# Complement masks of five tiles of a graph attention head made by accumulating DMAs, a new order of tiles on TensorE, and a fourth comparison on VectorE in every other head

## What is computed

```python
seq = (x @ W_seq).reshape(N, H, DH)                     # N = 2048, H = 16, DH = 32
score1 = jnp.einsum('nhd,d->hn', seq, a1)
score2 = jnp.einsum('nhd,d->hn', seq, a2)
scores = leaky_relu(score1[:, :, None] + score2[:, None, :], negative_slope=0.2)
scores = scores + (1.0 - adj)[None, :, :] * MASK_VAL
attn = softmax(scores, axis=-1)
hidden = jnp.einsum('hij,jhd->ihd', attn, seq).reshape(N, D_IN)
x = x + elu(hidden @ W_out + b_out)
```

## Time and profile before

| | |
|---|---|
| median of 3 runs | 1165.29 us (1164.87 to 1166.19) |
| the profiled execution | 1169.42 us, span of its instructions 1167.0 us |
| heads of the second layer | from about 635 to 1096 us of the span |
| busy share of the span, PE, DVE, ACT, POOL | 93%, 81%, 69%, 14% |

### The profile page before, as it was taken

How to read it: one execution, slowest core, us unless ns; L and a number is a source line. 1 busy time by engine, 2 the same in 40 slices (tenths; PEclk the granted TensorE clock), 3 DMA queues, 4 the chain that set the end, 5 groups by cost and what they waited for, 6 DMA issues and landing times. The chain is left out here.

```text
span 1167.0 us, 24746 instructions
## 1 busy us (share of the span) xinstructions
PE 1080.7 (93%) x10565; PEld 738.8 (63%) x10565; DVE 949.3 (81%) x1323; ACT 809.0 (69%) x843; POOL 163.1 (14%) x174
## 2 busy tenths in 40 slices
PE   1999986999999999999996999999999999999997
PEld 1444432444444444444443999999999999999743
DVE  2355336899999999998834899999999999999565
ACT  1334326677777777775525999999999999999122
POOL 2788640000000000000000100100110000000011
PEclk9999996999999999999997899999999999999999
DMA  9630452322221121000433011110111111111311
GB/s 340 142 26 2 110 104 68 75 57 66 66 66 43 42 57 57 28 37 27 163 126 131 38 38 38 38 39 38 38 38 38 39 38 38 38 39 38 110 72 72
DMA packets 38269, 77.69 MB, mean 67 GB/s; under 512 B 5653, under 2 KB 15250, under 8 KB 36114
## 3 DMA queue, kind: packets, MB, share of 16 engines
q1 hardware_dynamic: 31954, 67.62, 16.1%
q0 software_dynamic: 6208, 8.50, 6.0%
HBM read 65.39 MB, written 23.21 MB: 76 GB/s over the span
## 5 line engine op out<-in xcount | busy, mean ns | idle before, releaser
L1443 ACT ACTIVATE area_h<-area_a,keep 128x2048 fp8e4<-128x2048 f32 x208 | 396.9, 1987 | 0.5 <-PEq L1577 0.5
L1595 PE MATMUL psum<-s_V,area_h 128*128 128x99 bf16 x2560 | 254.5, 210 | 21.1 <-issue 10.9
L1595 PEld LDWEIGHTS psum<-s_V,area_h 128*128 128x128 fp8e4 x2560 | 237.4, 98 | 25.2 <-issue 22.8
L1598 PE MATMUL psum<-s_V,area_h 128*128 128x198 bf16 x1536 | 218.7, 249 | 0.0
L1599 PE MATMUL psum<-s_V,late 128*128 128x99 bf16 x1536 | 212.8, 209 | 0.0
L1596 PE MATMUL psum<-s_V,area_b 128*128 128x99 bf16 x2048 | 205.5, 210 | 0.0
L1596 PEld LDWEIGHTS psum<-s_V,area_b 128*128 128x128 fp8e4 x2048 | 190.3, 98 | 0.0
L737 PE MATMUL psum<-area_h,f_region 128*128 128x512 f32 x384 | 184.9, 596 | 0.0
L1493 DVE TENSOR_TENSOR area_h<-area_h,area_a 128x512 uint32<-128x512 uint32 x256 | 173.5, 688 | 9.1 <-ACT area_h L1443 4.6
L1159 DVE SCALAR_TENSOR_TENSOR f_region<-area_b,s_r,f_region 128x1500 f32<-128x1500 f32 x96 | 170.8, 1780 | 2.2
L1170 DVE CUSTOM_DVE_ANT_0 area_b<-psum,late 128x1500 f32<-128x1500 f32 x96 | 161.1, 1715 | 10.8 <-PE psum L652 10.6
(11 more groups left out here) (175 smaller groups left out, 1343.5 us busy)
## 6 DMA issues: line engine op xcount, KB each, us to landing
area_a<-s_rows SPq DMA_DIRECT2D x16, 1024.0 KB, 4.6
rel_planes<-f_h SPq DMA_DIRECT2D x3, 2304.0 KB, 15.9
late<-rel_planes SPq DMA_DIRECT2D x36, 192.0 KB, 2.6
area_h<-in_x SPq DMA_DIRECT2D x4, 1024.0 KB, 12.9
keep<-in_adj POOLq DMA_DIRECT2D x16, 256.0 KB, 6.6
f_region<-in_x SPq DMA_DIRECT2D x16, 256.0 KB, 4.7
x<-f_region SPq DMA_DIRECT2D x16, 256.0 KB, 2.0
area_a<-adj_chunks SPq DMA_DIRECT2D x4, 1024.0 KB, 9.1
```

What stands on the lines that cost most here:

```text
L1443: act.activation(masks[:, j, :], s1b[:, b, :], ACT.Relu, bias=t["s2"][:, n, 0, j:j + 1], scale=BIG, saturate=False).then_inc(signs, 1)
L1595: pe.matmul(out[:, :, 0:DZ], masks[:, j, cols], V[:, b, j, :, 0:DZ], **first)
L1598: pe.matmul(out, masks[:, j, cols], V[:, b, j, :, :], **first)
```

## The change

The set FAR of tiles with a complement of their own grows from ten to twelve. Five of them (0, 2, 6, 8, 11) no longer get it from VectorE: a plain copy of the adjacency tile is laid out in `fars`, and GpSimd issues a DMA that adds the mask to it as 16-bit integers. 0x40 + 0x40 = 0x80 in a byte is minus zero, 0x40 + 0 stays 2.0, so the sum is the complement. Since the DMA overwrites the copy, SP loads it anew for each head from memory (`far_rows`), once TensorE has used the tile (begin_far). VectorE makes the complements of tiles 1, 7, 9, 12 and 14, GpSimd those of 3 and 5 as before. TensorE takes the tiles in the order of TURN instead of 0 to 15; the mask of tile j is still made in the order of j. In odd heads VectorE compares four tiles (2, 6, 10, 14) instead of three. The stage ahead writes four tiles of `nadjT` and five copies of adjacency tiles, and SP stores those five to `far_rows`.

```diff
+            for d, j in enumerate(DMA_FAR):
+                sp.wait_ge(t["apart"], d + 1)
+                sp.dma_start(t["far_rows"][d], t["fars"][FAR.index(j)]).then_inc(t["far_begun"][d], 16)
             heads.sync(sp)
...
             dve.wait_ge(masked, HA * ET)
+            dve.wait_ge(w_ready, ET)
             for i, j in enumerate(NEAR_TILES):
                 dve.tensor_scalar(t["nadjT"][:, i, :].bitcast(U32).rearrange("p (t i) -> p t i", t=NT),
                                   t["adjT"][:, :, j, :].bitcast(U32), SIGNS, None, ALU.bitwise_xor).then_inc(t["lasting"], 1)
+            for j in DMA_FAR:
+                dve.tensor_scalar(t["fars"][FAR.index(j)].bitcast(U32).rearrange("p (t i) -> p t i", t=NT),
+                                  t["adjT"][:, :, j, :].bitcast(U32), 0, None, ALU.bitwise_or).then_inc(t["apart"], 1)
...
-VECTOR_SIGN = (3, 8, 13)
-FAR = (0, 1, 3, 5, 6, 7, 9, 11, 13, 14)
+SIGN_TILES = ((3, 8, 13), (2, 6, 10, 14))
+FAR = (1, 3, 5, 7, 9, 12, 14, 0, 2, 6, 8, 11)
 POOL_FAR = (3, 5)
-VECTOR_FAR = tuple(j for j in FAR if j not in POOL_FAR)
+DMA_FAR = (0, 2, 6, 8, 11)
+VECTOR_FAR = tuple(j for j in FAR if j not in POOL_FAR + DMA_FAR)
+TURN = (1, 3, 4, 5, 0, 7, 2, 9, 10, 12, 6, 13, 8, 14, 15, 11)
...
-            for n in range(HB - 2):
-                sp.wait_ge(mask_ready, NT * (n + 1))
-                load(n + 2, n % 2)
+
+            def begin_far(n, d):
+
+                place = TURN.index(DMA_FAR[d])
+                if place < NT - 1:
+                    sp.wait_ge(mask_used, (NT - 1) * (n + 1) + place + 1)
+                else:
+                    sp.wait_ge(psum_done[1], n + 1)
+                sp.dma_start(fars[FAR.index(DMA_FAR[d])], t["far_rows"][d]).then_inc(far_begun[d], 16)
+            for n in range(HB - 1):
+                for d in range(len(DMA_FAR) - 1):
+                    begin_far(n, d)
+                if n < HB - 2:
+                    sp.wait_ge(mask_ready, NT * (n + 1))
+                    load(n + 2, n % 2)
+                begin_far(n, len(DMA_FAR) - 1)
...
-                for j in POOL_FAR:
+                for j in sorted(POOL_FAR + DMA_FAR):
                     pool.wait_ge(mask_ready, NT * n + j + 1)
-                    complement(pool, j, ALU.subtract).then_inc(pool_far, 1)
+                    if j in POOL_FAR:
+                        complement(pool, j, ALU.subtract).then_inc(pool_far, 1)
+                    else:
+                        d = DMA_FAR.index(j)
+                        pool.wait_ge(far_begun[d], 16 * (n + 1))
+                        pool.dma_start(fars[FAR.index(j)].bitcast(U16), masks[:, j, :].bitcast(U16), accum_op=ALU.add).then_inc(far_added[d], 16)
...
-                    if j not in VECTOR_SIGN:
-
-                        if j < NT - 1:
-                            act.wait_ge(mask_used, (NT - 1) * n + j + 1)
+                    if j not in SIGN_TILES[n % 2]:
+
+                        if TURN.index(j) < NT - 1:
+                            act.wait_ge(mask_used, (NT - 1) * n + TURN.index(j) + 1)
                         elif n > 0:
                             act.wait_ge(psum_done[1], n)
...
-                    if j + 1 in VECTOR_SIGN:
+                    if j + 1 in SIGN_TILES[n % 2]:
                         vector_sign(n, b, j + 1)
...
-            def step(n, b, half, j):
-
-                base = 4 * half
-                if j == 0:
+            def step(n, b, half, place):
+
+                base, j = 4 * half, TURN[place]
+                if place == 0:
                     pe.wait_ge(bank_free[half], n + 1)
                 pe.wait_ge(mask_ready, NT * n + j + 1)
                 if j in POOL_FAR:
                     pe.wait_ge(pool_far, len(POOL_FAR) * n + POOL_FAR.index(j) + 1)
+                elif j in DMA_FAR:
+                    pe.wait_ge(far_added[DMA_FAR.index(j)], 16 * (n + 1))
                 elif j in FAR:
                     pe.wait_ge(far_ready, len(VECTOR_FAR) * n + VECTOR_FAR.index(j) + 1)
```

## The result

The changed kernel takes **1177.16 us** (median of 4 runs, 1175.48 to 1180.18), the kernel before 1165.08 beside it (1164.46 to 1166.19): a ratio of 1.0097, 95% interval 1.0069 to 1.0126. The forecast was 1171.5 in a range of 1164 to 1179, slower. The sign and the path that sets a head's time came true. The forecast's own sum was 6.25 us, so 5.8 of the 12.1 us were not in it.

The account below looks back on a forecast made before the run. VectorE's work sum bounded the kernel at 28.21 us a head; after the change a loop of 28.51, taken as 28.535, would. First head, fourteen loops (399.49) and last head gave 6.25 later: 1165.29 + 6.25 = 1171.5 us, range 1164 to 1179.

Parts of the forecast that it names:

- the loop over tile 12's complement: Second reduction, VectorE's way to that complement, TensorE's remaining steps, next second reduction: 28.51 us a head; forecast's chance 0.66.
- rival (d): In the heads, VectorE's operations lengthen beside five times the DMA traffic: 5% is 0.6 us a head, 1180; chance 0.06.
- second path: First half's full PSUM, first reduction and masks delay the second reduction: 0.03 to 0.05 us more in half the heads.
- TensorE's gaps: Waits on VectorE's complements: about 1.2 us at place 5 (even heads), 1 at 7 (odd), 1.3 to 1.5 at 9.
- Rival (a): Engines' work sums set the heads, 0.8 to 1.2 us less each: 1148 to 1154 us; chance 0.13.
- tile 7's loop: Even heads, from second reduction over tile 7's complement and TensorE's remaining steps to the next: 27.27 us.
- tile 9's loop: From second reduction over tile 9's complement and TensorE's remaining steps to the next: 26.99 us.
- The accumulating DMA: GpSimd's mask-adding DMA in the heads: taken as 6.6 us, free up to 11.7, no gain from landing early.
- What follows it is not changed: Everything behind the last reduction, up to the kernel's end, was claimed to take the same time: nothing added.
- Head 0: First head, no reductions: TensorE waits for tile 12's complement; second reduction at 676.82 instead of 675.89.
- Head 15: Last head, no take-offs: 10.36 + 0.82 + 14.79 + 0.20 = 26.17 us to the last reduction.
- Stores and copies in the stage ahead: Before the heads, VectorE's three more copies and SP's five stores: costed at nothing, perhaps a microsecond or two once.

Follow-up runs that it names:

- reduce_later: Changed kernel with VectorE's second reduction behind mask 7 of the next head instead of mask 5; 1186.00 us, ratio 1.0156 to the kernel before.
- the swap: Changed kernel with only tiles 12 and 6 exchanged in TensorE's order; 1158.32 us, ratio 0.9926 to the kernel before.

## Why the prediction was right, and where it was short

- **Which path sets the head: right.** No engine's sum, but the loop over tile 12's complement. Forecast 12.70 + 0.82 + 14.79 + 0.20 = 28.51; measured 12.82 (857.66 - 844.84), 0.82 (to 858.48) and 14.98 (to 873.46), 28.62, and 28.60 on average. Fourteen heads: 399.49 forecast, 400.40 measured. The 0.12 in the first term is one comparison of 1.40 us instead of 1.28. Ten comparisons of this trace begin 0.2 us after GpSimd has begun to issue a DMA, and all ten take 1.39 to 1.44; 24 others meet an issue otherwise and keep 1.28. That is rival (d) in small, by the issue and not by the traffic.
- **Not seen: the loop through the first reduction**, 28.68, which ties with it. The forecast had it only as a "second path" that costs 0.03 to 0.05. The time came out the same, but advice drawn from the one loop alone (reduce_later) promised at least twice what both loops leave.
- **TensorE's gaps: right in place**, at 5 in even heads, 7 in odd ones and 9 in both, and nearly so in size: 1.10 for about 1.2, 0.88 for about 1, and at place 9 1.35 in odd and 1.09 in even heads for 1.3 to 1.5. VectorE idles 1.93 us in one head and 0.89 in the next, forecast 2.1 and 0.9.
- **Rival (a), the sums decide, is excluded** by the changed kernel, **and is nearly what the swap gives**, 27.36. But the forecast had its two halves wrong. It gave 27.27 in even heads, by tile 7's loop, and 27.60 in odd ones. In the swap it is 27.60 from an even head to an odd one, by VectorE's sum, which is above tile 7's loop there, and 27.15 from an odd head to an even one, by tile 9's loop (forecast 26.99).
- **The accumulating DMA: bounded rightly.** Landing took 3.5 us, where the value taken was 6.6 and the room 12.3. In the order of the change no step waited for it; in the order 0 to 15 it was late. The estimate of 3.8 worked out from the Trainium skill (DMA: Bandwidth & Descriptors, Anatomy of one DMA — SWDGE (gpsimd) path) was the nearer. The warning of the Trainium skill (SBUF — State Buffer, SBUF: two separate sides) about GpSimd's descriptors is borne out in kind and not in size: ten of the eighty issues grew from 0.86 to 1.70 us and ended 0.1 us after the comparison that they met, none to five times its length. The prediction took 0.6 us for an issue; nothing in this order hung on the difference.

```profile
late<-area_h POOLq DMA_DIRECT2D x64, 256.0 KB, 3.5
```

```profile
848.98 1.70 POOL L1454 DMA_DIRECT2D late<-area_h  x1 [0.33 <-DVE area_h L1525]
```

- **"What follows it is not changed": wrong, 4.2 us.** The instructions are not, but GpSimd's closing drain depends on how many DMAs it issued in its last block (since its drain at 577 us in before and at 571 in after). This is the largest part of the miss, a term that the sum put at nothing.
- **Head 0: 0.93 forecast, 0.99 where the clock held**, and 1.6 more where TensorE's clock fell after its stop; the rest of its 3.8 is the wait for the row of s1, which the kernel before has too when its stage ahead ends on time.
- **Head 15**: 26.17 forecast, 26.38 measured. **Stores and copies in the stage ahead**: no cost found. The stretch ended earlier than before's, by luck, and its step at 594.65 to 599.23 in the kernels with the change lies where it does in those without (596.23 to 599.40), so that a cost of a microsecond can't be told from no cost.

Summed: 0.99 in head 0, 6.75 in fourteen loops, -0.31 in head 15 and 4.23 in the drain are 11.7, and up to 13.3 with the clock's 1.6; the medians differ by 12.1. It is luck that a term of 4.2 us that the sum did not have fits into the room above the forecast; the own range of the prediction, 1167.6 to 1175, was missed by 2.2 us.

## What to carry to other kernels

When an order of tiles is changed, sum the closed path from the point where two engines meet to where they meet again, through *every* such point, and not only each engine's work: here one tile one place too early cost 17 us, while every engine had got less work. A DMA moved to GpSimd has a price also at the end of the kernel if GpSimd is the last to finish; let another queue issue the last stores, and the drain lies beside other work. Before moving an instruction to break a loop, look for the second loop of the same length and for what the instruction kept apart.

## What the runs showed of the hardware that was not expected

- GpSimd's drain at the end of its block: 1.36 us in the kernel before, 4.64 with 40 and 7.90 with 80 more plain DMAs (the 80 alike with 2 KB and with 256 KB); with 80 accumulating ones more 5.61. Per plain DMA of the block, the sixteen stores counted in, it is 82 to 85 ns.
- An accumulating DMA of 256 KB within SBUF lands 3.5 us after its issue, which holds GpSimd for 0.86 us (plain: 0.56 for 256 KB, 0.49 for 2 KB).
- A GpSimd complement of 1.28 us costs VectorE 1.07 us when its masks run beside it and 1.02 when a comparison does, and takes 1.65 itself; beside a reduction from PSUM both keep their length.
- A comparison of VectorE that begins 0.2 us after GpSimd has begun to issue an accumulating DMA takes 1.40 us instead of 1.28, and the issue 1.70 instead of 0.86.
